# A routed expert block on one core: the expert tiles begin inside the token loop, ScalarE squares from the row sum and stores the first residual, GpSimd makes the negative mean

## What is computed

```python
x = x + tanh(g_xattn[0]) * attn(ctx, ctx, mask, key_mask, layernorm(x), Wq, bq, Wk, bk)
x = x + tanh(g_ffn[0])   * moe(layernorm(x), Wg, W1, W2, W3, bias)

# attn: softmax((q k^T) * 128**-0.5 * layernorm(x), with masks)
# moe:
routing_weights = sigmoid(x @ Wg.T)
_, top_k_index = top_k(routing_weights + bias, 2)
h1 = einsum('th,efh->tef', x, W1)
h3 = einsum('th,efh->tef', x, W3)
g = silu(h1) * h3 * expert_w[:, :, None]
out = einsum('tef,ehf->th', g, W2)
```

## Time and profile before

| what | value |
|---|---|
| median of 3 runs | 326.88 us (326.1 to 329.94) |
| profiled execution | 325.86 us |
| its span | 323.9 us |
| PE (TensorE matmul) busy | 279.9 us, 86% |
| DVE (VectorE) busy | 191.4 us, 59% |
| ACT (ScalarE) busy | 127.3 us, 39% |
| POOL (GpSimd) busy | 196.5 us, 61% |
| mean granted TensorE clock | 0.919 of full |
| moved by DMA | 48.69 MB, mean 150 GB/s |

### The profile page before, as it was taken

How to read it: one execution, slowest core, us unless ns; L and a number is a source line. 1 busy time by engine, 2 the same in 40 slices (tenths; PEclk the granted TensorE clock), 3 DMA queues, 4 the chain that set the end, 5 groups by cost and what they waited for, 6 DMA issues and landing times.

```text
span 323.9 us, 5197 instructions
## 1 busy us (share of the span) xinstructions
PE 279.9 (86%) x1316; PEld 203.7 (63%) x1316; DVE 191.4 (59%) x505; ACT 127.3 (39%) x239; POOL 196.5 (61%) x208
## 2 busy tenths in 40 slices
PE   3699799487997696988999996999999999999980
PEld 1145364253354584866888775888888888888860
DVE  2698777899598977598345425444535445454530
ACT  2678569133566652222233222333332332333220
POOL 5188897618777777557776448465646445653313
PEclk9979989655599679999999999999999999999997
DMA  7999898783353361546464657666767556766435
GB/s 230 317 397 328 270 329 301 255 301 138 127 170 133 92 192 34 100 69 101 93 121 76 97 99 112 111 117 110 143 95 124 108 83 115 134 126 97 46 54 65
DMA packets 27026, 48.69 MB, mean 150 GB/s; under 512 B 9524, under 2 KB 10296, under 8 KB 25976
## 3 DMA queue, kind: packets, MB, share of 16 engines
q0 software_dynamic: 9760, 20.49, 36.1%
q1 hardware_dynamic: 14408, 15.04, 14.5%
q10 hardware_dynamic: 2832, 12.85, 11.7%
HBM read 28.51 MB, written 19.85 MB: 149 GB/s over the span
## 4 chain that ended last, share of the span: by engine, by line
DMA 45%; issue 19%; POOL 11%; PE 10%; DVE 9%; ACT 3%; POOLq 2%; SPq 1%; ACTq 0%; DVEq 0%
DMA out<-rows,slot 30%; DMA out<-rows 10%; POOL out L460 4%; POOL rows L441 4%; PE bank L902 2%; DMA rows<-in_x 2%; POOL slot_table L428 2%; POOLq L452 2%; DVE w_lo L841 1%; DMA w_hi<-in_ctx_t 1%; DVE rows L698 1%; DMA rows<-xn_rows,slot 1%; DVE w_hi L675 1%; PE bank L909 1%; PE bank L981 1%
## 5 line engine op out<-in xcount | busy, mean ns | idle before, releaser
L460 POOL DMA_INDIRECT out<-rows,slot x39 | 62.3, 1598 | 65.4 <-DMA out<-rows,slot 42.1
L993 PE MATMUL bank<-w_hi,xt_hi 128*128 x156 | 64.7, 414 | 0.0
L994 PE MATMUL bank<-w_lo,xt_hi 128*128 x156 | 61.1, 392 | 0.0
L995 PE MATMUL bank<-w_hi,xt_lo 128*128 x156 | 61.0, 391 | 0.0
L820 DVE TENSOR_TENSOR xt_lo<-bank,xt_hi 128x512 fp32r<-128x512 f32 x39 | 26.9, 690 | 50.7 <-ACT xt_hi L584 50.7
L592 ACT ACTIVATE rows<-bank 128x256 f32<-128x256 f32 x39 | 15.0, 384 | 88.1 <-PE bank L995 88.1
L441 POOL DMA_INDIRECT rows<-xn_rows,slot x39 | 39.2, 1005 | 16.2 <-issue 10.2
L605 ACT ACTIVATE rows<-bank,slot 128x512 f32<-128x512 f32 x39 | 26.8, 687 | 50.0 <-PE bank L1022 39.0
L428 POOL DMA_INDIRECT slot_table<-entry,slot_index x32 | 33.1, 1034 | 17.8 <-DVE slot_index L783 9.0
L826 DVE SCALAR_TENSOR_TENSOR rows<-rows,bank 128x256 f32<-128x256 f32 x39 | 16.4, 420 | 38.7 <-ACT rows L592 38.5
L1020 PE MATMUL bank<-w_hi,gt_hi 128*128 x78 | 30.9, 396 | 4.8 <-DVE gt_lo L837 4.8
(11 more groups left out here) (131 smaller groups left out, 454.6 us busy)
## 6 DMA issues: line engine op xcount, KB each, us to landing
w_lo<-in_w ACTq DMA_DIRECT2D x8, 1024.0 KB, 7.6
xn_rows<-w_hi SPq DMA_DIRECT2D x17, 256.0 KB, 6.8
rows<-in_x SPq DMA_DIRECT2D x16, 256.0 KB, 4.3
out<-rows SPq DMA_DIRECT2D x16, 256.0 KB, 3.9
w_lo<-in_w ACTq DMA_DIRECT2D x8, 512.0 KB, 4.5
w_hi<-in_ctx_t SPq DMA_DIRECT2D x4, 256.0 KB, 5.3
slot<-slot_table SPq DMA_DIRECT2D x39, 1.0 KB, 2.2
rows<-xn_rows,slot POOLq DMA_INDIRECT x39, 4.3
```

Of the source, the lines that this page charges most:

```text
L460: pool.indirect_dma_start(out=out[0:SPARE + P * READY[segment(i)], :], out_offset=bass.IndirectOffsetOnAxis(ap=slot[:, i, 0:1].bitcast(U32 ...
L993: pe.matmul(ps_h[i % 2][:], xt_hi[:, i % 2, k, :], hi, start=(k == 0), stop=False)
L994: pe.matmul(ps_h[i % 2][:], xt_hi[:, i % 2, k, :], lo, start=False, stop=False)
L995: mm = pe.matmul(ps_h[i % 2][:], xt_lo[:, i % 2, k, :], hi, start=False, stop=(k == KC - 1))
```

## The change

Five things are changed together; the kernel computes the same.

- VectorE's L701 goes. GpSimd makes `nmean2` in `normed`; `squares` takes the row sum itself as bias with a scale of -512, so that its sum is 512 squared too large, which `row_scales` takes back (`1 / D ** 3`).
- The stores of x1 go from SP's queue to ScalarE's, right behind `squares` (`store_x1` in ScalarE's program). SP no longer has that store behind its wait.
- The projection's copies stand behind the exponentials of the next step, and its matmuls stand ahead on the TensorE, in the place of that step's spin.
- The slots of group 0 are made one step sooner, its scatters run in steps 8 to 11 in place of 9 to 12, and the expert tiles begin inside the token loop: the gathers 0 and 1 in GpSimd's step 14, and the first hidden layer ahead of the logits and transposes of the last tiles. In place of that, `router_weights(1)`, `router_slots(1)` and the positions of group 1 move behind the first expert tiles.
- Buffers and PSUM banks are assigned anew, and the tables of splits, loads and scatters are new. VectorE has 16 low splits in both.

```diff
-    LOADS = {0: (2,), 1: (3,), 2: (4,), 4: (5,), 5: (6,), 6: (7,), 7: (8,), 8: (9, 10, 11), 9: (12,), 10: (13,), 11: (14,),
-             12: (15,)}
+    LOADS = {1: (2,), 2: (3,), 4: (4,), 5: (5,), 6: (6,), 7: (7,), 8: (8, 9), 9: (10, 11), 10: (12,), 11: (13,), 12: (14,),
+             13: (15,)}
-    LATE_SCATTERS = {0: (1, 6, 8), 4: (2, 0, 2), 5: (2, 2, 3), 6: (2, 3, 5), 7: (2, 5, 6), 8: (2, 6, 8), 9: (2, 8, 9),
-                     10: (2, 9, 10)}
+    LATE_SCATTERS = {0: (1, 0, 6), 1: (1, 6, 8), 5: (2, 0, 2), 6: (2, 2, 4), 7: (2, 4, 5), 8: (2, 5, 7), 9: (2, 7, 8),
+                     10: (2, 8, 10)}
...
@@ GpSimd
+                pool.tensor_scalar(nmean2[:, col], sum2[:, col], -1.0 / D, None, ALU.mult).then_inc(s_nmean, 1)
+                pool.wait_ge(s_nmean, tile + 1)
...
-            gather(0)
-            gather(1)
+                if step == TILES - 2:
+                    gather(0)
+                    gather(1)
+            gather(2)
             row_scales(TILES)
             normed(TILES - 1)
-            gather(2)
             gather(3)
-            enter_slots(1, 0, 6)
...
@@ ScalarE
-                act.wait_ge(s_nmean, tile + 1)
-                act.activation(ps_s[tile % 2][:], x_row(tile), ACT.Square, bias=nmean2[:, t:t + 1],
+                act.wait_ge(s_x1, tile + 1)
+                act.activation(ps_s[tile % 2][:], x_row(tile), ACT.Square, bias=sum2[:, t:t + 1], scale=-float(D),
                                accum_out=sqsum2[:, t:t + 1]).then_inc(s_sq, 1)
+
+            def store_x1(tile):
+                act.wait_ge(s_x1, tile + 1)
+                act.dma_start(out[SPARE + tile * P:SPARE + (tile + 1) * P, :], x_row(tile)).then_inc(s_x1_out[tile % XR], 16)
...
@@ VectorE, expert tiles
-            router_ranks(1)
-            router_weights(1)
-            gathered_lo(0)
-            router_slots(1)
-            gathered_lo(1)
+            gathered_lo(0)
+            gathered_lo(1)
...
                 if i == 0:
+                    router_weights(1)
+                elif i == 1:
+                    router_slots(1)
+                elif i == 2:
                     list_tiles(1)
...
@@ TensorE, expert tiles
                 if i == 0:
-                    logits(TILES - 1)
+                    logits(TILES - 3)
+                    transpose(TILES - 2)
                     gathered(2)
                 elif i == 1:
                     gate_transpose(0)
+                    logits(TILES - 2)
+                    transpose(TILES - 1)
                     gathered(3)
                     output(0, last)
                     gate_transpose(1)
+                    logits(TILES - 1)
+                    positions(1)
```

More of the change, by code:

```diff
@@ L90, in flamingo_routed_block @@
         xg = rows[:, 0:XG]
-        y = rows[:, XG:XG + 2]
-        gate = rows[:, XG + 2].rearrange("p (r s) -> p r s", r=2)
+        gate = rows[:, XG].rearrange("p (r s) -> p r s", r=2)
+        y = rows[:, XG + 1:XG + 3]
         xt_hi = sb("xt_hi", [P, 2, KC, P], F32R)
@@ L295, in x_row, with prob @@
             return rows[:, (tile + 2) % XR]
+        def prob(tile):
+            return x_row(TILES - 4) if tile >= TILES - 2 else prob_sb
         def normed_row(tile):
-            if tile == TILES - 1:
-                return x_row(TILES - 3)
-            return early(15, 1) if tile % 2 == 0 else early(13, 1)
+            if tile >= TILES - 2:
+                return x_row(tile)
+            return xn_even if tile % 2 == 0 else xn_odd
         def normed_columns(tile):
-            row = x_row(TILES - 2) if tile == TILES - 1 else early(12, 1)
+            row = x_row(tile) if tile >= TILES - 2 else xt_sb
             return row.rearrange("p (k s) -> p k s", k=KC)
@@ L531, in exponentials @@
                 act.wait_ge(s_nb, tile + 1)
[L532 removed]
+                act.activation(ps_s[tile % 2][:], prob(tile), ACT.Exp, bias=nbias[:, t:t + 1],
                                scale=rstds[:, t, 0:1], accum_out=prob_sum[:, t:t + 1]).then_inc(s_exp, 1)
@@ L630, in _ @@
                 exponentials(step)
+                if step % NT == 3 and step // NT + 1 < B:
+                    project(step // NT + 1)
+                if step == TILES - 1:
+                    gathered_hi(0)
+                    gathered_hi(1)
                 if step >= 2:
                     transposed(step - 2)
-                for unit in units_in(step)[0:2]:
-                    if unit != 2 * E + 4:
-                        split_hi(unit)
+                for unit in units_in(step):
+                    split_hi(unit)
                 if step == END[0] + 1:
@@ L678, in scores @@
                 dve.wait_ge(s_neg, tile + 1)
-                dve.tensor_tensor_reduce(prob, prob, ps_neg[:], 1.0, LOWEST, ALU.add,
+                dve.tensor_tensor_reduce(prob(tile), prob(tile), ps_neg[:], 1.0, LOWEST, ALU.add,
                                          ALU.max, zmax[:, t:t + 1]).then_inc(s_zmax, 1)
```

155 lines of the change are left out of this document (74 added, 81 removed).

## The result

The changed kernel takes 338.69 us (median of four, 335.64 to 341.87) against 327.01 for the kernel before (four runs, 326.1 to 329.94). The ratio is 1.031, with a 95% interval of 1.020 to 1.042. Ratios here leave disturbed executions out, so they can differ a little from the ratio of two medians. The profiled execution took 337.88 us, with a span of 336.1. The forecast was 329.5, range 320.5 to 336.0.

The account below looks back on a forecast made before the run. The prediction took the chain of adds, hanging on add 0 and group 1's slots, to decide when the full TensorE stage begins. Add 0 2.0 us later plus 1.5 made +3.5 on 325.86: forecast 329.5 us, range 320.5 to 336.

Parts of the forecast that it names:

- First half: Token loop up to x1 of tile 8: earlier x1 stores and the moved projection save 4.5 us, ends -9 and 0.
- the rival with the store behind weights: Token loop: x1 stores queue behind weights, so the first-half gain is 0; T = 107.4, time 334; chance 0.17.
- Second half: Token loop, x1 of tile 8 to that of tile 15: 1.6 us less than 49.6, ends -4 and 0.
- new banks and buffers: New assignment of PSUM banks and buffers: claimed to cost nothing.
- T: End of x1 of tile 15, late in the token loop; forecast at 102.9 us.
- T to first scatter: From x1 of tile 15's end to group 1's first scatter: 18.6 us instead of 8.8, ends 17 and 22.
- First scatter to add 0: Group 1's first scatter to the first add on GpSimd: 12.2 us instead of 13.8, with nine transfers left of ten.
- Add 0 to add 10: Chain of adds in the expert tiles: 1.5 us longer as group 2's scatters move, ends 0 and +2.
- The end follows add 10: Last stage: the TensorE is full behind add 10, so the end moves with it, +3.5 us.
- Low clock in the first hidden layers: Rival: the clock stays low through the first hidden layers, 6 us of it seen, time 335; chance 0.1.
- the chain of adds giving way: Rival in the expert tiles: the adds catch up, some 8 us of the earlier hidden layer count, time 318; chance 0.12.
- The sum: All terms together: +2.0 at add 0 and +1.5 make +3.5 us on 325.86, forecast 329.5.

Follow-up runs that it names:

- b2: The kernel before with only the x1 stores moved from SyncE's queue to ScalarE's, behind the squares; 326.13 us, ratio 0.993.
- b3: The kernel before with only the projection's order changed: matmuls ahead of the logits in place of the spin, copies behind the next exponentials; 329.25 us, ratio 1.001.
- e3: The changed kernel with group 0's scatters one step later (steps 9 to 12) and ScalarE's split 19 moved to step 14; 331.39 us, ratio 1.011.
- e1: The changed kernel with group 0's scatters in GpSimd's steps 9 to 12 and not 8 to 11; 336.55 us, ratio 1.029.
- e5: e3 with the low split of unit 8 on GpSimd and that of unit 9 on VectorE, not the other way round; 333.67 us, ratio 1.016.
- e7s: e3 with the before kernel's tables for splits, weight loads and GpSimd's low splits, and 8 spinning matmuls a step, not 5; 334.87 us, ratio 1.016.
- e4: The changed kernel with weights, slots and positions of group 1 ahead of gate 0, not behind gates 0 and 1; 336.88 us, ratio 1.029.

## Why the prediction was wrong, step by step

- **First half, -4.5 us: right in size, in part by other means.** Measured -3.4. The free step of VectorE went from 4.00 to 3.82 us, and the stores landed in 3.8 us (median), not near 8 as the rival with the store behind weights has it. The Trainium skill (DMA: Bandwidth & Descriptors, Queues, rings and completion order) speaks for that rival. The traces show at most 0.7 us for the place behind a weight: 4.6 in b2, against 3.9 in the kernel before. Other transfers took longer in b2: loads of x landed in 5.3 us (4.3 before), weights of 512 KB in 7.0 (4.5). b2 gives 4.3 for the store alone. The projection, which the term counts too, gives nothing in b3. And the half has two low splits less (2.4 us of VectorE), which the prediction didn't count.
- **Second half, -1.6 us with ends -4 and 0: wrong, +8.3.** This is the step that failed, and it missed by 9.9 us. The prediction summed instructions of VectorE, as if VectorE set the pace. Even that sum was off: it has one low split more, for the loop as a whole, where this half has three more (twelve and not nine). Its terms with a number make -2.5; the 0.9 us up to -1.6 stand for ScalarE's stores, and no row gives them. Above all it didn't look at who stands in line on GpSimd: the table of scatters was read for the adds, not for the normed rows behind them (A). It costed "new banks and buffers" at nothing without naming what each reused buffer now waits for; one waits for a store that SyncE issues late (B). e3 puts A and B at 5.2 us; without them tiles 10 to 15 are 0.8 us faster than before, with one low split more in them. Tiles 8 and 9 take 3.9 us more: one of the three low splits (1.2 us), the hold (2.1 us), and the tanh (1.0 us) are 4.3, the shorter steps give a little back.
- **T to first scatter, 8.8 to 18.6: right** (19.0, and 17.6 to 20.1 in e1 to e3, e5 to e7s). Its parts were off both ways: the first hidden layer began at T + 2.6 and not T + 0.9, as TensorE waited for the gathers, the positions followed 13.1 us behind it (14 forecast) and the scatter 3.3 behind them (3.7). **First scatter to add 0, 12.2: right** (11.5).
- **Add 0 to add 10, +1.5 us: wrong in sign, -1.3.** Of small weight. The step that it priced was right: add 8 to add 9 took 5.79 us (5.8 forecast, 4.52 before). But add 0 to add 8 took 42.6 us and not 45.0. That ten adds are no constant e4 shows, with 60.2.
- **The end follows add 10: right.** In all seventeen traces the end is 134.5 to 137.3 us behind it, over T from 106.96 to 117.21.
- **Low clock in the first hidden layers, and the chain of adds giving way**: neither. The first hidden matmuls took 0.79 and 0.63 us and from 119.02 on 0.39, so the low clock lasted some 3 us of them, about what the forecast's term holds (1 to 1.5). The granted clock played elsewhere too, ahead of the tanh.
- **The sum** was made on the profiled execution (325.86). On the median of before it would be 330.4, which changes nothing here.

The loss of 12.2 us in the profiled execution is thus 4.9 at T and 6.6 from T to add 10 (the forecast's own terms made this 9.7), with 0.7 behind. The late group 1 and the early begin cost about what was forecast or less; the loop that should have paid for them lost as well. The negative mean on GpSimd is 0.4 per cent by itself, at the edge of what can be measured.

## What to carry to other kernels

When a stage has no full engine, don't sum the work of the busiest one: take each in-order queue, and for each instruction that a table moves into it write down what waits behind it and who waits for that. For a new buffer layout list every reuse with the last reader or transfer that it has to wait for, and where that transfer stands in its own queue. When tables of work change, count what each stage gets and not the total: VectorE had 14 low splits for 13 in the loop, but 12 for 9 in its second half. And follow a gain through the stage behind it: the store on ScalarE won 4.3 us by tile 8 and had 1.3 left at the end of the loop, as most of the rest went in one step, in which VectorE then met a late tanh and a split of GpSimd.
